# Half-size weight transfers with a limit on how many are under way, weight bounds moved from VectorE to ScalarE, and later exchanges in other ticks, in a kernel that runs an RNN and an LSTM together

## The reference

```python
def _L0_cond_ref(x, h0, Wx, Wh, b):          # simple RNN, 512 -> 512
    xW = jnp.einsum('ntd,dh->nth', x, Wx) + b
    def step(prev_h, xw):
        next_h = jnp.tanh(prev_h @ Wh + xw)
        return (next_h, next_h)

def _L1_cond_ref(x, h0, Wx, Wh, b):          # LSTM, 512 -> 4*512 gates
    def step(carry, xw_t):
        prev_h, prev_c = carry
        a = xw_t + prev_h @ Wh
        i, f, o = sigmoid of the first three quarters of a, g = tanh of the last
        next_c = f * prev_c + i * g
        next_h = o * jnp.tanh(next_c)

x = x + _L0_cond_ref(x, cond_1024, L0_Wx, L0_Wh, L0_b)
x = x + _L1_cond_ref(x, cond_1024, L1_Wx, L1_Wh, L1_b)
```

## Time and profile before

| | |
|---|---|
| median of 3 runs (lowest, highest) | 864.72 us (861.84, 864.87) |
| time of the profiled execution | 864.07 us |
| its span | 862.0 us |
| mean granted TensorE clock | 0.994 |
| busy | PE 98%, DVE 80%, ACT 63%, POOL 37% |
| DMA in the first twentieth of the span | over 0.8 of 16 engines busy |
| chain that ended last | PE 85%, DVE 8%, ACT 3%, issue 3% |

### The profile page before, as it was taken

How to read it: one execution, slowest core, us unless ns; L and a number is a source line. 1 busy time by engine, 2 the same in 40 slices (tenths; PEclk the granted TensorE clock), 3 DMA queues, 4 the chain that set the end, 5 groups by cost and what they waited for, 6 DMA issues and landing times.

```text
span 862.0 us, 51618 instructions
## 1 busy us (share of the span) xinstructions
PE 840.9 (98%) x22590; PEld 619.0 (72%) x22590; DVE 685.6 (80%) x1886; ACT 546.6 (63%) x1509; POOL 319.4 (37%) x677
## 2 busy tenths in 40 slices
PE   7999999999999999999999999999999999999996
PEld 6565655565677777777777777777777777777885
DVE  5688988898778887878787887878887887777765
ACT  2555346565567766767677766766776767767642
POOL 1211156632244334343434333443434343434320
PEclk9899999999999999999999999999999999999999
DMA  8901001110011101011111001111100000000000
GB/s 319 272 2 27 12 19 28 27 28 7 24 29 29 29 18 26 16 29 28 29 29 26 20 18 27 28 29 29 29 19 18 24 17 16 16 16 16 16 14 18
DMA packets 40192, 30.66 MB, mean 36 GB/s; under 512 B 5772, under 2 KB 38688, under 8 KB 38688
## 3 DMA queue, kind: packets, MB, share of 16 engines
q1 hardware_dynamic: 39712, 27.27, 11.3%
q10 hardware_dynamic: 256, 0.11, 0.0%
HBM read 18.95 MB, written 8.39 MB: 32 GB/s over the span
## 4 chain that ended last, share of the span: by engine, by line
PE 85%; DVE 8%; ACT 3%; issue 3%; DMA 0%; ACTq 0%; POOL 0%; DVEq 0%; POOLq 0%
PE ps_l L1130 32%; PE ps_l L1201 26%; PE ps_r L1270 8%; PE ps_r L1289 8%; PE ps_l L1178 3%; PE ps_l L1143 2%; PE ps_l L1167 1%; PE ps_r L1253 1%; ACT gates L701 1%; PE ps_r L1243 1%; DVE pre_l L949 1%; DVE ig L958 1%; DVE c L960 1%; PE ps_l L1318 1%; PE ps_l L1100 1%
## 5 line engine op out<-in xcount | busy, mean ns | idle before, releaser
L458 POOL TENSOR_TENSOR xb<-xb,h_l 128x128 f32<-128x128 f32 x127 | 59.2, 466 | 421.5 <-DVE h_lo L991 418.7
L701 ACT ACTIVATE gates<-pre_l 128x256 f32<-128x256 f32 x128 | 53.4, 417 | 119.0 <-DVE pre_l L949 118.9
L1130 PE MATMUL ps_l<-whl_hi,hT_hi 128*32 128x512 f16 x1888 | 123.0, 379 | 1.0 <-DVE whl_lo L921 0.9
L1130 PE MATMUL ps_l<-whl_lo,hT_hi 128*32 128x512 f16 x1888 | 123.0, 379 | 0.0
L1130 PE MATMUL ps_l<-whl_hi,hT_lo 128*32 128x512 f16 x1888 | 123.0, 379 | 0.0
L1201 PE MATMUL ps_l<-wxl_hi,wxl_raw 128*32 128x256 f16 x2400 | 115.0, 273 | 2.5 <-ACT wxl_raw L649 2.0
L1201 PE MATMUL ps_l<-whl_raw,wxl_raw 128*32 128x256 f16 x3600 | 115.9, 273 | 0.0
L1201 PEld LDWEIGHTS ps_l<-whl_raw,wxl_raw 128*32 128x32 f16 x3600 | 96.8, 97 | 11.6
L949 DVE SCALAR_TENSOR_TENSOR pre_l<-ps_l,g_products,bias_l 128x256 f32<-128x256 f32 x140 | 60.5, 472 | 49.9 <-PE ps_l L1130 43.9
L713 ACT ACTIVATE h_r<-pre_r 128x128 f32<-128x128 f32 x128 | 39.6, 310 | 92.4 <-DVE pre_r L1008 61.5
L1130 PEld LDWEIGHTS ps_l<-whl_lo,hT_hi 128*32 128x32 f16 x1888 | 51.5, 97 | 50.6
(11 more groups left out here) (154 smaller groups left out, 1926.5 us busy)
## 6 DMA issues: line engine op xcount, KB each, us to landing
xb<-in_x SPq DMA_DIRECT2D x128, 64.0 KB, 2.3
out<-xb SPq DMA_DIRECT2D x124, 64.0 KB, 1.8
whl_raw<-in_L_cond_Wh SPq DMA_DIRECT2D x4, 1024.0 KB, 13.3
wxl_raw<-in_L_cond_Wx SPq DMA_DIRECT2D x4, 1024.0 KB, 17.7
wxr_raw<-in_L_cond_Wx SPq DMA_DIRECT2D x1, 1024.0 KB, 5.9
whr_raw<-in_L_cond_Wh SPq DMA_DIRECT2D x1, 1024.0 KB, 7.8
out<-xb SPq DMA_DIRECT2D x4, 48.0 KB, 1.7
wxl_raw<-peaks SPq DMA_DIRECT2D x5, 2.0 KB, 1.9
```

The lines of the kernel that those rows point to most:

```text
L458: nc.gpsimd.tensor_tensor(xb[g % NX][:, t, :], xb[g % NX][:, t, :], h_l[s % 2][:, :], ALU.add).then_inc(out_done, 1)
L701: nc.scalar.activation(gates[:, 0:2 * P], pre_l[:, 0:2 * P], ACT.Sigmoid).then_inc(lstm_act, 1)
L1130: last = nc.tensor.matmul(ps_l[s % 4][quarter(j), :], (hT_hi, hT_lo)[h_part][:, k, :], gate_slice(whl[w_part][k], j), start=False, stop=(h ...
```

## The change

Eight edits, all in one step:

1. **Transfers.** Each chunk of WhL and WxL comes as two halves of 0.5 MB with a semaphore each. SP waits for the half three ahead of it before it issues the next, so that at most three halves are under way. WxR is SP's first transfer; x group 0 is issued by ACT, ahead of h0 and the biases. x groups 3 to 7 wait for the last chunks of WxL.
2. **Bounds.** The bound of WhR (tick 0) and of WhL 1 (tick 1) move from DVE to ACT, to ticks 2 and 1; those of WhL 2 and 3 go one tick later, to 3 and 4.
3. **Exchange of the RNN weights' peaks** (R_SCALE_AT) from tick 1 to tick 3; its scale chain on DVE from tick 3 to tick 4.
4. **Exchange of the WhL peaks.** PE's turn_peaks and DVE's spread move from the end of tick 4 into tick 5, where spread_peaks and the scale chain are.
5. **Bias of the LSTM** spread by PE ahead of the first products. These become 2 products of 512 columns instead of 16 of 128.
6. **step_0_input** is cut in four: chunk 0 ahead of the RNN's step 6, chunk 1 behind it, chunks 2 and 3 at the end of tick 6.
7. **Exchanges by transfer** one tick earlier (row reduced in tick 4g - 6, scales in 4g - 5); SP sends the reduced row right behind the row.
8. **pair_third** of the last pairs waits for u2_out behind the first of its two block products.

```diff
-        R_SCALE_AT = 1
+        R_SCALE_AT = 3
-        BATCH_AT = [10, 12] + [TG * g - 6 for g, _ in BATCHES[2:]]
+        BATCH_AT = [10, 12] + [TG * g - 6 for g, _ in BATCHES[2:BY_PRODUCT]] + [TG * g - 7 for g, _ in BATCHES[BY_PRODUCT:]]
-        W_MAX_AT = {1: (OF_H, 1), 5: (OF_X, 0)}
+        W_MAX_AT = {5: (OF_X, 0)}
-        W_BOUND_AT = {0: [(OF_H, 0)], 2: [(OF_H, 2)], 3: [(OF_H, 3)], 6: [(OF_X, 1)], 7: [(OF_X, 2)], 8: [(OF_X, 3)]}
+        W_BOUND_AT = {0: [(OF_H, 0)], 1: [(OF_H, 1)], 3: [(OF_H, 2)], 4: [(OF_H, 3)], 6: [(OF_X, 1)], 7: [(OF_X, 2)], 8: [(OF_X, 3)]}
-        FIRST_PRODUCTS = 16
+        FIRST_PRODUCTS = 2
...
-            load_x(sp, 0)
+            def load_chunk(of, k, two_ahead, ahead):
+                rows = chunk_rows((WhL, WxL)[of], k)
+                sp.wait_ge(two_ahead, DMA)
+                sp.dma_start(raw[of][k][:, 0:GH // 2], rows[:, 0:GH // 2]).then_inc(s_half[of][k], DMA)
+                sp.wait_ge(ahead, DMA)
+                sp.dma_start(raw[of][k][:, GH // 2:GH], rows[:, GH // 2:GH]).then_inc(s_rest[of][k], DMA)
             sp.dma_start(wr_raw[OF_X][:, :], WxR.rearrange("(p k) n -> p (k n)", k=J)).then_inc(s_wr[OF_X], DMA)
             sp.dma_start(wr_raw[OF_H][:, :], WhR.rearrange("(p k) n -> p (k n)", k=J)).then_inc(s_wr[OF_H], DMA)
-            load_chunk(whl_raw[0][:, :], WhL, 0, s_whl[0])
-            load_chunk(whl_raw[1][:, :], WhL, 1, s_whl[1])
+            load_chunk(OF_H, 0, s_wr[OF_X], s_wr[OF_X])
+            load_chunk(OF_H, 1, s_wr[OF_H], s_half[OF_H][0])
             load_x(sp, 1)
...
+            sp.wait_ge(s_rest[OF_X][2], DMA)
             load_x(sp, 3)
+            sp.wait_ge(s_rest[OF_X][3], DMA)
...
-                if g in ROW_BEHIND:
-                    peaks_to_row(ROW_BEHIND[g])
-                if g in WIDE_BEHIND:
-                    peaks_to_all(WIDE_BEHIND[g])
+                if g in EXCHANGE_BEHIND:
+                    peaks_to_row(EXCHANGE_BEHIND[g])
+                    peaks_to_all(EXCHANGE_BEHIND[g])
...
         def _(act):
+            load_x(act, 0)
...
+            def rnn_weight_bound():
+                act.wait_ge(s_wr[OF_H], DMA)
+                nc.scalar.activation(wr[OF_H][1][:, :].bitcast(BF16), wr_raw[OF_H][:, :], ACT.Abs,
+                                     accum_out=peaks[:, R_PEAK + OF_H:R_PEAK + OF_H + 1]).then_inc(r_peaked, 1)
...
+                if k == R_SCALE_AT - 1:
+                    rnn_weight_bound()
...
             def pair_third(p):
-                pe.wait_ge(u2_out, p + 1)
-                block_product(p, 2, ALL[:3])
+                if pair_step(p) < S3:
+                    pe.wait_ge(u2_out, p + 1)
+                    block_product(p, 2, ALL[:3])
+                else:
+                    block_product(p, 2, ALL[:3])
+                    pe.wait_ge(u2_out, p + 1)
                 block_product(p, 5, ALL, m5_mm)
...
+            pe.wait_ge(s_bias_l, DMA)
+            nc.tensor.matmul(ps_l[1][:, :], spread_j, bias_rows_l, start=True, stop=True).then_inc(bias_mm, 1)
             for _ in range(FIRST_PRODUCTS):
-                nc.tensor.matmul(ps_l[1][:, 0:P], ident[:, :], ident[:, :], start=True, stop=True)
+                nc.tensor.matmul(ps_l[2][:, :], ident[:, :], ident[:, :].unsqueeze(1).broadcast_to([P, J, P]), start=True, stop=True)
...
+                if k == LAG - 1:
+                    step_0_input(0)
                 if k < LAG:
                     recurrent_r(k)
+                if k == LAG - 1:
+                    step_0_input(1)
+                if k == SCALE_AT[OF_H]:
+                    pe.wait_ge(w_peaked[OF_H], J)
+                    pe.wait_ge(r_step, 1)
+                    turn_peaks(EXCHANGE[OF_H], slice(0, J))
```

More of the change, by code:

```diff
@@ L168, in rnn_lstm_kernel @@
         s_bias_l = sem("bias_l_loaded")
-        s_whl = [sem(f"whl_loaded{k}") for k in range(J)]
-        s_wxl = [sem(f"wxl_loaded{k}") for k in range(J)]
+        s_half = [[sem(f"{w}_half_loaded{k}") for k in range(J)] for w in ("whl", "wxl")]
+        s_rest = [[sem(f"{w}_rest_loaded{k}") for k in range(J)] for w in ("whl", "wxl")]
         x_in = [sem(f"x_loaded{i}") for i in range(NX)]
@@ L372, in input_product_done, with chunk_loaded @@
                 eng.wait_ge(xl_mm, s)
+        def chunk_loaded(eng, of, k):
+            eng.wait_ge(s_half[of][k], DMA)
+            eng.wait_ge(s_rest[of][k], DMA)
         def x_loaded(eng, g):
@@ L389, in _ @@
         def _(sp):
-            def load_chunk(dst, w, k, loaded):
-                sp.dma_start(dst, chunk_rows(w, k)).then_inc(loaded, DMA)
-            load_x(sp, 0)
+            def load_chunk(of, k, two_ahead, ahead):
[4 more added lines that the diff above has]
+                sp.dma_start(raw[of][k][:, GH // 2:GH], rows[:, GH // 2:GH]).then_inc(s_rest[of][k], DMA)
             sp.dma_start(wr_raw[OF_X][:, :], WxR.rearrange("(p k) n -> p (k n)", k=J)).then_inc(s_wr[OF_X], DMA)
             sp.dma_start(wr_raw[OF_H][:, :], WhR.rearrange("(p k) n -> p (k n)", k=J)).then_inc(s_wr[OF_H], DMA)
-            load_chunk(whl_raw[0][:, :], WhL, 0, s_whl[0])
-            load_chunk(whl_raw[1][:, :], WhL, 1, s_whl[1])
+            load_chunk(OF_H, 0, s_wr[OF_X], s_wr[OF_X])
+            load_chunk(OF_H, 1, s_wr[OF_H], s_half[OF_H][0])
             load_x(sp, 1)
-            load_chunk(whl_raw[2][:, :], WhL, 2, s_whl[2])
-            load_chunk(whl_raw[3][:, :], WhL, 3, s_whl[3])
+            load_chunk(OF_H, 2, s_rest[OF_H][0], s_half[OF_H][1])
+            load_chunk(OF_H, 3, s_rest[OF_H][1], s_half[OF_H][2])
             load_x(sp, 2)
-            for k in range(J):
-                load_chunk(wxl_raw[k][:, :], WxL, k, s_wxl[k])
+            load_chunk(OF_X, 0, s_rest[OF_H][2], s_half[OF_H][3])
+            load_chunk(OF_X, 1, s_rest[OF_H][3], s_half[OF_X][0])
+            load_chunk(OF_X, 2, s_rest[OF_X][0], s_half[OF_X][1])
+            load_chunk(OF_X, 3, s_rest[OF_X][1], s_half[OF_X][2])
+            sp.wait_ge(s_rest[OF_X][2], DMA)
             load_x(sp, 3)
+            sp.wait_ge(s_rest[OF_X][3], DMA)
             for g in range(4, NX):
@@ L572, in _ @@
             nc.scalar.activation(bias_r, ps_l[0][:, 0:P], ACT.Copy).then_inc(bias_done, 1)
+            act.wait_ge(bias_mm, 2)
+            nc.scalar.activation(bias_l[:, :], ps_l[1][:, :], ACT.Copy).then_inc(bias_done, 1)
             def x16_hi(g):
@@ L751, in _ @@
                     seed_r(k + 2)
-                if k == BIAS_L_AT:
-                    act.wait_ge(bias_mm, 2)
-                    nc.scalar.activation(bias_l[:, :], ps_l[1][:, :], ACT.Copy).then_inc(bias_done, 1)
                 if R0 - 1 <= k < T - 1:
@@ L1044, in _ @@
                         turn_x(TURN_X_AT[k])
-                    if k == SCALE_AT[OF_H] - 1:
-                        spread(EXCHANGE[OF_H], J)
                 if 0 <= k - LAG:
@@ L1097, in step_0_recurrent @@
                 for k in chunks:
-                    pe.wait_ge(s_whl[k], DMA)
+                    chunk_loaded(pe, OF_H, k)
                     for j in range(J):
@@ L1101, in step_0_recurrent, with step_0_input @@
                                          start=(k == 0), stop=False)
-            def step_0_input():
+            def step_0_input(k):
                 pe.wait_ge(yT_done, 1)
-                for k in range(J):
-                    pe.wait_ge(s_wxl[k], DMA)
-                    for j in range(J):
-                        last = nc.tensor.matmul(ps_l[0][quarter(j), :], yT[0][:, k, 0, :], gate_slice(wxl_raw[k], j),
-                                                start=False, stop=(k == J - 1))
-                last.then_inc(lstm_mm, 1)
+                chunk_loaded(pe, OF_X, k)
+                for j in range(J):
+                    last = nc.tensor.matmul(ps_l[0][quarter(j), :], yT[0][:, k, 0, :], gate_slice(wxl_raw[k], j),
+                                            start=False, stop=(k == J - 1))
+                if k == J - 1:
+                    last.then_inc(lstm_mm, 1)
             def recurrent_l(s):
@@ L1354, in _ @@
                     turn_peaks(EXCHANGE_R, slice(R_PEAK, R_PEAK + 2))
-                if k == BIAS_L_AT:
-                    pe.wait_ge(s_bias_l, DMA)
-                    nc.tensor.matmul(ps_l[1][:, :], spread_j, bias_rows_l, start=True, stop=True).then_inc(bias_mm, 1)
                 if k - 1 == R_SCALE_AT:
@@ L1361, in _ @@
                     step_0_recurrent(STEP_0_AT[k])
-                if k + 1 == SCALE_AT[OF_H]:
-                    pe.wait_ge(w_peaked[OF_H], J)
-                    pe.wait_ge(r_step, 1)
-                    turn_peaks(EXCHANGE[OF_H], slice(0, J))
                 if k == LAG - 1:
-                    step_0_input()
+                    step_0_input(2)
+                    step_0_input(3)
                 elif 1 <= k - LAG + 1 < S2:
```

25 lines of the change are left out of this document (11 added, 14 removed).

## The result

The changed kernel takes 865.71 us in the median of 20 runs, the kernel before 862.94 in 20 runs on the same chip: the ratio is 1.0031, with a 95% interval of 1.0022 to 1.0041. It is slower by 1.9 to 3.5 us, where 2.5 less was forecast. The profiled execution took 865.63 with a span of 863.7. Against that of before (864.07, which itself lay 1.1 above the median of the 20) it lost 1.6.

The account below looks back on a forecast made before the run. PE, busy 98%, bounds the kernel; only start, exchanges and end can gain. 1.3 + 0.5 + 0.65 = 2.5 less than 864.07 gives 861.6, stated as 861.8; range 858.5 to 866.5.

Parts of the forecast that it names:

- Part 1: Start of the kernel up to T0: LSTM's bias landed at 8.5 plus 6.4 of work gives 14.9, against 12.96 before.
- T0: Mark in the start: DVE adds the bias of RNN step 0; 12.96 before, forecast 14.9.
- rival of late x and biases: Start: x group 0 and biases come late, T0 19.5, start 3.3 worse, total 866.2; chance 0.16.
- Part 2: T0 to Y, RNN steps 0 to 5: 14.5 instead of 17.1, between 13.8 and 16, half the fetch and clock losses gone.
- Y: Mark in the start: DVE adds the bias of RNN step 5; 30.04 before, forecast 29.4.
- Part 3: Y to the gates: 11.4 before, Y + 10.7 after, gain 0.7 from the new order of DVE's and ACT's work.
- the gates: Mark in the start: the LSTM's first gates on ACT, at 41.43 before; behind them the same instruction order in both kernels.
- The weights don't: Start: loading the weights doesn't set its length; last WxL chunk lands at 36.7, its products run from 37.15 without a gap.
- Start in all: Whole start: 30.04 - 29.4 + 0.7, a gain of 1.3.
- Exchanges: Steady part: five exchanges one tick earlier shorten PE's waits; gain 0.5, at most 1.0, -0.5 if the row comes late.
- End: Ticks 129 and 131: first block's products, 0.33 each time, run under PE's wait for u2; gain 0.65.
- Tick 9: PE arrives some 2.6 us before DVE and ACT and waits longer than 0.94; otherwise they don't set the start's end.

Follow-up runs that it names:

- biases_first: The changed kernel with x group 0 issued behind h0 and the biases, still on ACT's queue; ratio to the kernel before 1.0040.
- small_packets: The changed kernel with WxR and WhR loaded in four column quarters each, in packets of 2 KB instead of 8; 864.80 us in one run.
- x0_on_sp: The changed kernel with x group 0 moved back to SP's queue, ahead of WxR; ratio to the kernel before 1.0039.
- bounds_on_dve: The changed kernel with x group 0 first on SP, five halves under way, bounds of WhL 1 and WhR back on DVE with their exchanges; ratio to before 0.9968.
- before_2_5_mb: The kernel before with only the transfers changed: weights in halves, five (2.5 MB) under way, x group 0 first on SP; ratio to before 0.9979.
- x0_on_sp_2_5_mb: The changed kernel with x group 0 first on SP's queue and five halves (2.5 MB) under way instead of three; ratio to the kernel before 0.9983.
- no_first_products: The changed kernel without its two unused first products; ratio to the kernel before 1.0012.
- before_bounds_on_act: The kernel before with only the bounds of WhL 1 and WhR moved to ACT, with their exchanges; 866.93 us against 862.68, ratio 1.0051.

## Why the prediction was wrong

The time fell into the range and on the other side of no change. Its steps, in order:

**Part 1, up to T0: both terms too small, and the first step that failed.** The rival of late x and biases is what came: it had 866.2 with T0 at 19.5, in the class from 865 to 868.5 with a chance of 0.16, and 865.71 was measured. The biases were to be in at 8.5; the RNN's reached PE at 11.53, and PE began with the LSTM's at 12.09. The prediction had written down the case in which each packet of ACT's queue waits for one of the weights, ending at about 13, and then took a value near the other end. The counts above show one-for-one turns up to 8 us, and they delay x group 0; for the biases behind it the two kernels biases_first (10.64) and small_packets (11.86) show that more than the turns holds them back, and what it is stays open. The second term is the work behind the landing: 6.4 was put down, and from 12.09 to 20.83 it took 8.7, since PE worked at half speed up to 19.4, not only at its beginning. T0 at 20.83 lies beyond the 19.5 of that rival. The statement that the shorter first products win nothing was too kind: behind a late bias they cost 2.9, as the run without them shows.

The Trainium skill ("DMA: Bandwidth & Descriptors", section on queues, rings and completion order) has an engine drain a packet of 9 to 17 descriptors of one queue before it turns to the next. The counts of 112 to 112 and 320 to 304 between 4 and 6 us fit a turn after each single packet of the profile, and so differ from what the prediction made of that rule.

**Part 2, T0 to Y: near the number, where the chunks are in time.** 13.67 against 14.5, just under the lower bound of 13.8. The stops for instructions and the low clock are gone, and the runs without the limit put the throttle's part at 2.7 to 2.8. But the stage has a limit that the prediction left out. In x0_on_sp, where T0 is 13.09 and WxR is issued behind x group 0 as in the kernel before, it took 16.33, since ACT waited 3.0 for chunks of WhL. In after the late T0 hides that; whether 13.67 would also hold at the prediction's own T0 of 14.9, no run shows.

**Part 3, Y to the gates: right number, wrong reason.** 10.20 against 10.7. But the 11.39 of the kernel before weren't the order of its work. Its row of RNN step 6 in the earlier trace rows says that DVE was idle for 2.07 behind PE, and PE was at half clock from 33.0 on. Where the clock isn't low behind Y, the old order takes 9.2 to 9.4 (bounds_on_dve, before_2_5_mb) and the new one 10.2 to 10.3 (after, x0_on_sp_2_5_mb, no_first_products, and before_bounds_on_act, which has it in the kernel before). The step "gain 0.7" should have read "cost 1.0". It took a disturbed row as the price of an order.

**"The weights don't": this is the step that failed for the change as a whole.** It is true of the kernel before, where 14.8 + 21.9 = 36.7 is when the last chunk lands and the products start at 37.15. That is a margin of 0.45. The prediction let the last half land before 35, that is, 36.7 less the 1.9 by which WxR is issued earlier: it put the limit's price on loading at nothing. It should have asked what rate 1.5 MB holds: a half took 5.5 to land, and three of them in each 5.5 make under 290 GB/s, an estimate. The windows of five us from 20 to 40 have 211, 314, 270 and 311 GB/s in after; in the kernel before those from 15 to 35 have 303 to 413. WxL landed at 41.2. In after the late bias hides this; with x group 0 back on SP it costs, with WhL's late chunks, all that the earlier T0 would bring (1.0039). With five halves and all else alike the ratio is 0.9983.

**Start in all** (to pre_l of step 2): forecast 1.3 less, measured 3.0 more. **Exchanges:** 0.16 instead of 0.5, and PE's waits at L1289 are as before. **End:** 1.1 instead of 0.65; PE's wait fell by 0.7 in two ticks, and the rest of the gain isn't assigned to a row. **Tick 9:** PE idle 2.1, where it was to be there some 2.6 early, so the claim that DVE and ACT set the end of the start held, and no low clock followed.

Of the marks named in advance, T0 after 17.5 and the WxL half after 35 were the ones that spoke against the forecast, and both did.

## What to carry over

A limit on what is under way has a right depth, not a direction: three halves of 0.5 MB starved the DMA engines, four or five kept them full from 15 to 35 us and left no stop of 1 us for instructions, and without a limit PE stopped for up to 2.2 us. Work it out as bytes under way over the time from issue to landing, and compare with the rate the unthrottled kernel has. A resource with a margin of 0.45 us isn't free to be slowed; and when two chains end within 2 us of each other, undoing one can show nothing until the other is undone too. Small transfers that the first instruction needs are issued ahead of the large ones in time: a second queue didn't save them from the large ones (4.8 against 10.6 to 11.9 us).

## What was new about the hardware

- Two queues with work were served packet by packet in turn between 4 and 6 us, 112 to 112 with 8 KB against 0.5 KB packets and 320 to 304 with 2 KB against 0.5 KB, so a queue of small packets gets 6% of the bytes in the one case (0.05 of 0.84 MB) and 19% in the other (0.14 of 0.72 MB). From 8 to 10 us the counts part (359 to 73 in small_packets).
- A transfer of 2 KB on a second queue took 2.3 us to reach PE with little ahead of it, 7.2 (issue at 4.03 + 0.29, PE at 11.53) beside a full queue with the limit, 8.4 in biases_first (issue at 1.94 + 0.31, PE at 10.64), and about 13 without the limit (issue at 4.12 + 0.29, PE at 17.63).
- After 11.5 us without a product PE worked at half speed for 8 us, up to 19.4, and in x0_on_sp, where it stood idle for 2.3 us up to 38.66, the clock was at 0.50 from 38.4 on for 6.8 us.
